# All short matmuls of a step behind its four projections, in a gated recurrent block with a feed-forward gate

## The chip, the cores and the metric

The kernel runs on one core of a Trainium2 chip. Its time is the device time of one execution in microseconds. The time before is the median of three executions. A separate execution was profiled, and every start time and duration below comes from that one.

## The reference

One sequence of 2048 tokens with 512 features goes through a layer norm. An attention-like branch `s` and a feed-forward gate `g` are computed from the normed input, and the output is `x + s * g`. Cut to what matters:

```python
q, k, v = (_causal_dwconv(_silu(x @ W), conv_w) for W, conv_w in ...)  # 4 taps; 16 heads x 128
z, a, b = x @ Wz, x @ Wa, x @ Wb
q, k = rope(q), rope(k)
q = q / max(norm(q), 1e-12);  k = k / max(norm(k), 1e-12)
for s in range(4):                           # each token and the three before it
    attn = einsum('bshd,bshd->bsh', q, lag(k, s)) * scale
    out += (attn * sigmoid(lag(a, s) * b))[..., None] * lag(v, s)
s = (out * rsqrt(mean(out * out) + eps) * norm_w * silu(z)) @ Wout
g = silu(relu(x @ sign(up).T * up_scale) @ sign(down).T * down_scale * output_scale)
```

## The kernel before

**Three stages.** A setup normalizes and transposes x and splits it into a coarse part `x_hi` and a remainder `x_lo`. The attention stage then goes over 16 heads of 128 features. In each head it goes over 4 chunks of 512 tokens. The feed-forward and the output projection follow. Each engine has its own program, written out by hand, and semaphores order them; no scheduler is involved.

**Steps.** The attention stage has one *step* for each head and chunk, counted by `c = h * 4 + g` from 0 to 63, and three more steps that empty the pipeline. A step works on four chunks at once: the newest one, and those one, two and three steps back (`back(h, g, k)`). `front` says that there is a newest chunk, so it is true up to c = 63.

**TensorE in a step**, in the order before:

1. transposes of q and of k of the chunk one step back, 4 of 128x128 each (L829), q into `bank_tqv` and k into `bank_tk`;
2. projections of q and k of the newest chunk. Each projection is a *series* of 12 matmuls of 512 columns on split weights (L771);
3. `turn_v`: 4 transposes of v of the chunk one step back into `bank_tqv` (L798);
4. the projection of v;
5. `sum_values`: the sum of values of the chunk three steps back, 4 or 5 plain fp32 matmuls of up to 132 columns (L808, L813). The trace records each of these as two instructions;
6. the projection of z for the chunk two steps back;
7. two *picks* of 32 columns (L889, L890) and the *scores*, 4 fp32 matmuls of 132 columns (L897, again two records each), for the chunk two steps back.

**The bank that is used twice.** `bank_tqv` holds the transposed q at the start of a step and the transposed v later. ScalarE takes the squares of q out of it for the norms (L556), then `turn_v` may write (`norms_done`), then ScalarE copies the transposed v to `v_tok` (L566). The next step's transposes of q wait for that copy (`v_tok_done`, L824).

**ScalarE in a step**, in the order before: the norms (L556), silu and first convolution tap of q and of k (L521 to L536), the copy to `v_tok` (L566), silu and tap of v, the squares of the summed values (L579), silu of z (L590). In the last chunk of a head it also splits the next head's weights of q, k and v (L516), and in chunk 1 those of z. In step 1 alone it computes a tanh of the gates (L584) ahead of what follows.

**The other engines.** VectorE does the convolutions (L638), the rotation (L648 to L655), the coefficients (L711 to L737) and the gated output (L732). GpSimd computes the inverse norms and `rq_parts`, for which the picks wait (L431 to L445), splits weights (L406), and issues the transfer that adds up the squares (L458).

Of the kernel before, what the change touches and what calls it, by code (L numbers as in the profile page):

```python
# [150 lines left out]
def attention(nc, env):  # L151
# [18 lines left out]
    with ExitStack() as ctx:  # L170
# [4 lines left out]
        v_tok = sb("v_tok", [P, NB, D], at=ctx)  # L175
# [12 lines left out]
        out_sq = sb("out_sq", [P, CH], at=ctx)  # L188
        o_buf = sb("o_buf", [P, 2, CH], at=ctx)
        bank_qv, bank_kz = banks[0], banks[1]  # L190
        bank_tqv, bank_tk = banks[2], banks[3]
        bank_out, bank_rq = banks2
# [66 lines left out]
        turned_v = sem("turned_v", ctx)  # L259
        norms_done = sem("norms_done", ctx)  # L260
        v_tok_done = sem("v_tok_done", ctx)
# [12 lines left out]
        out_done = sem("out_done", ctx)  # L274
        out_sq_done = sem("out_sq_done", ctx)
# [3 lines left out]
        sq_added = sem("sq_added", ctx)  # L279
        block = ctx.enter_context(nc.Block())  # L280

        def back(h, g, k):

            h2, g2 = (h, g - k) if g >= k else (h - 1, g - k + G)
            if isinstance(h2, int) and not 0 <= h2 < H:
                return None
            return h2, g2
# [16 lines left out]
        def is_tail(h, g, step):  # L304

            return isinstance(h, int) and h == H and g == step
# [157 lines left out]
        def _(act):  # L464
# [78 lines left out]
            act.wait_ge(raw_in["z"], 16)  # L543
            nc.scalar.activation(w_hi["z"][:, :, :], raw["z"][:, :, :], ACT.Copy).then_inc(whi_done["z"], 1)

            def step(h, g):
                c = h * G + g
                front = back(h, g, 0)
                if at := back(h, g, 1):
                    g1 = at[1]  # L550
                    wait(act, turned_qk, c)
                    wait(act, rnorm_done, c - 2)
                    for i, bank in enumerate((bank_tqv, bank_tk)):
                        for b in range(BC):
                            block_of = bank[:, b * P:(b + 1) * P]
                            last = nc.scalar.activation(block_of, block_of, ACT.Square,  # L556
                                                        accum_out=norms[:, g1 % 2, i * BC + b:i * BC + b + 1])
                    last.then_inc(norms_done, 1)
                if front and not is_start(h, g):
                    silu_and_tap("q", bank_qv, h, g, c)  # L560
                    silu_and_tap("k", bank_kz, h, g, c)
                if at := back(h, g, 1):
                    g1 = at[1]
                    wait(act, turned_v, c)
                    wait(act, out_done, c - 3)
                    nc.scalar.activation(v_tok[:, g1 * BC:(g1 + 1) * BC, :],  # L566
                                         bank_tqv[:, :].rearrange("p (b d) -> p b d", b=BC),
                                         ACT.Copy).then_inc(v_tok_done, 1)
                if g == 3 and not is_last(h):
                    split_hi("q", h + 1, c)  # L570
                if front:
                    silu_and_tap("v", bank_qv, h, g, c)
                if g == 3 and not is_last(h):
                    split_hi("k", h + 1, c)
                    split_hi("v", h + 1, c)
                if back(h, g, 3):
                    wait(act, out_done, c - 2)
                    wait(act, sq_added, 16 * (c - 3))
                    nc.scalar.activation(out_sq[:, :], bank_out[:, :], ACT.Square).then_inc(out_sq_done, 1)  # L579
                if is_start(h, g - 1):  # L580
                    for i in range(2):
                        part = gate0[:, i * HALF_NB:(i + 1) * HALF_NB, :]
                        act.wait_ge(prod_done, i + 1)
                        nc.scalar.activation(part, part, ACT.Tanh, scale=0.5).then_inc(tanh_done, 1)  # L584
                if at := back(h, g, 2):
                    g2 = at[1]
                    wait(act, proj_done["z"], c - 1)
                    wait(act, o_done, c - 3)
                    bank = bank_qv if is_tail(h, g, 1) else bank_kz
                    nc.scalar.activation(z_act[:, g2 % 2, :], bank[:, :], ACT.Silu).then_inc(z_done, 1)  # L590
                if g == 1 and front and not (isinstance(h, int) and h == 0):
                    split_hi("z", h, c - 2)

# [149 lines left out]
        def _(pe):  # L743
# [33 lines left out]
            for b in range(NB):  # L777
                turn_x(b)
                half = range((b + 1) % 2 * TERMS // 2, ((b + 1) % 2 + 1) * TERMS // 2)
                at = (b + 1) // 2  # L780
# [13 lines left out]
            def turn_v(g1, c):  # L794
                wait(pe, norms_done, c)
                wait(pe, conv_done["v"], 3 * c)
                for b in range(BC):
                    last = nc.tensor.transpose(bank_tqv[:, b * P:(b + 1) * P],  # L798
                                               y["v"][:, g1 % 2, b * P:(b + 1) * P], ident)
                last.then_inc(turned_v, 1)  # L800

            def sum_values(g3, c):

                wait(pe, coef_done, c - 2)
                wait(pe, v_tok_done, c - 2)
                wait(pe, o_done, c - 3)
                if g3 > 0:
                    nc.tensor.matmul(bank_out[:, 0:LAGS], v_tok[:, g3 * BC - 1, :],  # L808
                                     coef[:, (g3 - 1) % 2, BC - 1, P:BW], start=True, stop=False,
                                     skip_group_check=True)  # L810
                for b in range(BC):
                    width = BW if b < BC - 1 else P
                    last = nc.tensor.matmul(bank_out[:, b * P:b * P + width], v_tok[:, g3 * BC + b, :],  # L813
                                            coef[:, g3 % 2, b, 0:width], start=(b == 0 and g3 == 0),
                                            stop=(b == BC - 1), skip_group_check=True)
                last.then_inc(out_done, 1)

            def step(h, g):
                c = h * G + g
                front = back(h, g, 0)  # L820
                at1, at2, at3 = (back(h, g, k) for k in (1, 2, 3))
                if at1:
                    g1 = at1[1]
# [20 lines left out]
                if front and not is_start(h, g):  # L844
                    wait(pe, z_done, c - 2)
                    project("k", bank_kz, h, g, c)
                if at1 and front:
                    turn_v(at1[1], c)
                if front:
                    wait(pe, silu_done["q"], 2 * c + 2)  # L850
                    project("v", bank_qv, h, g, c)
                if is_start(h, g):
# [2 lines left out]
                        last = nc.tensor.transpose(bank_ab[:, b * AB:(b + 1) * AB], ab_t[:, b * P:(b + 1) * P],  # L855
                                                   ident[0:AB, 0:AB])
                    last.then_inc(ab_turned, 1)
                if at3 and front:
                    sum_values(at3[1], c)
                if at2 and not is_tail(h, g, 1):  # L860
                    if front:
                        wait(pe, silu_done["k"], 2 * c + 2)
                    else:
                        wait(pe, z_done, c - 2)
                    project("z", bank_kz, at2[0], at2[1], c - 2)
                if at1 and not front:
                    turn_v(at1[1], c)
                if is_tail(h, g, 0):
                    wait(pe, silu_done["v"], 2 * c)
                    project("z", bank_qv, h - 1, G - 1, c - 1)  # L870
                    sum_values(at3[1], c)
# [8 lines left out]
                if at2:  # L880
# [14 lines left out]
                    for b in range(BC):  # L895
                        at = (g2 * BC + b) * P
# [452 lines left out]
```

## Time and profile before

| | us |
|---|---|
| median of three executions | 1412.47 (1412.08 to 1413.2) |
| the profiled execution, its own time | 1413.44 |
| its span, first to last instruction | 1411.6 |
| TensorE busy in the span | 1377.4 (98%) |
| VectorE / ScalarE / GpSimd busy | 1025.6 / 733.3 / 417.2 |

The attention stage fills the span from about 40 us to 982 us. In the timelines a line merges neighbouring instructions of one kind: its first start, the time from that start to the last one's end, and their count. Matmuls overlap in their records, since each passes through a pipeline. What a piece of work takes of TensorE's time is therefore read from its start to the start of the next piece, not from the duration.

### The profile page before, as it was taken

Reading aid. Unit: us, or ns where it says so; the run is one execution under the profiler, and the core shown is the slowest. Engines: PE = TensorE matmul, PEld = TensorE weight load, DVE = VectorE, ACT = ScalarE, POOL = GpSimd, SP = SyncE. Lnnn points to the kernel's source line nnn. Section 1 sums busy time; section 2 is a strip of 40 time slices with the busy share of each in tenths; the row PEclk is TensorE's granted clock in tenths of the full one; section 3 lists DMA queues with packets and bytes.
Section 4 is the critical chain, followed back from the end, with each engine's and each line's share of the span. In section 5 each row is a group of like instructions: output and inputs, shape, how many; then the busy total and the mean of one; then the engine's idle time right before and its main releaser. Section 6 shows DMA issues by size and latency. Waiting matters only on the chain. (4 is left out here: it accounts for less than half of the span.)

```text
span 1411.6 us, 23209 instructions
## 1 busy us (share of the span) xinstructions
PE 1377.4 (98%) x7048; PEld 1164.4 (82%) x7048; DVE 1025.6 (73%) x1597; ACT 733.3 (52%) x2146; POOL 417.2 (30%) x504
## 2 busy tenths in 40 slices
PE   6999999999999999999999999998899999999998
PEld 4778888888888888888888888886788888888886
DVE  7889999999999999999999999995113322234442
ACT  5655655556655556555565655553554444332221
POOL 6142443434434344444444444432000000000001
PEclk9999999999999999999999999999899999999999
DMA  9123333433344333443334333332431101065454
GB/s 303 38 70 88 90 83 97 99 87 89 79 100 102 75 97 74 104 97 78 93 74 111 89 82 89 82 83 72 137 120 53 45 22 45 25 185 171 142 170 157
DMA packets 103962, 137.60 MB, mean 97 GB/s; under 512 B 11248, under 2 KB 48112, under 8 KB 103664
## 3 DMA queue, kind: packets, MB, share of 16 engines
q1 hardware_dynamic: 94704, 120.28, 29.6%
q0 software_dynamic: 9216, 16.78, 7.0%
q8 instruction: 24, 0.39, 0.1%
q14 instruction: 18, 0.15, 0.0%
HBM read 61.53 MB, written 25.17 MB: 61 GB/s over the span
## 5 line engine op out<-in xcount | busy, mean ns | idle before, releaser
L431 POOL TENSOR_TENSOR rnorm<-norms,neg_half 128x8 f32<-128x8 f32 x64 | 126.2, 1971 | 366.4 <-DVE norms L663 366.4
L556 ACT ACTIVATE bank<-bank 128x128 f32<-128x128 f32 x512 | 133.7, 261 | 86.3 <-PE bank L829 86.3
L638 DVE SCALAR_TENSOR_TENSOR y_v<-u_v,cw_v,y_v 128x512 f32<-128x512 f32 x192 | 172.7, 899 | 6.8
L638 DVE SCALAR_TENSOR_TENSOR y_k<-u_k,cw_k,y_k 128x512 f32<-128x512 f32 x192 | 159.7, 832 | 16.5 <-ACT y_k L536 9.5
L1141 DVE TENSOR_TENSOR hid_lo<-relu,hid_hi 128x512 fp32r<-128x512 f32 x64 | 44.3, 693 | 172.3 <-ACT hid_hi L1087 172.3
L638 DVE SCALAR_TENSOR_TENSOR y_q<-u_q,cw_q,y_q 128x512 f32<-128x512 f32 x192 | 144.2, 751 | 30.0 <-ACT y_q L536 22.3
L1059 POOL TENSOR_TENSOR g_buf<-g_buf,up_raw 128x512 f32<-128x512 f32 x3 | 3.8, 1278 | 402.7 <-DVE g_buf L1162 402.7
L1182 DVE TENSOR_TENSOR hid_lo<-o_raw,hid_hi 128x512 fp32r<-128x512 f32 x64 | 44.3, 692 | 101.4 <-ACT hid_hi L1107 101.4
L1083 ACT ACTIVATE relu<-bank,us_sb 128x512 f32<-128x512 f32 x64 | 44.1, 689 | 121.7 <-PE bank L1222 121.7
L1107 ACT ACTIVATE hid_hi<-o_raw 128x512 fp32r<-128x512 f32 x64 | 40.5, 633 | 121.8 <-PE bank L1252 116.8
L1237 PE MATMUL bank<-down_sign,hid_hi 128*128 128x512 f32 x256 | 99.8, 390 | 0.9 <-DVE hid_lo L1141 0.9
L1252 PE MATMUL bank<-x_hi,hid_hi 128*128 128x512 f32 x256 | 99.7, 390 | 0.2 <-DVE hid_lo L1182 0.2
L1237 PE MATMUL bank<-down_sign,hid_lo 128*128 128x512 f32 x256 | 99.6, 389 | 0.0
L1252 PE MATMUL bank<-x_hi,hid_lo 128*128 128x512 f32 x256 | 99.6, 389 | 0.0
L1252 PE MATMUL bank<-x_lo,hid_hi 128*128 128x512 f32 x256 | 99.6, 389 | 0.0
L556 ACT ACTIVATION_READ_ACCUMULATOR bank<-bank 128x1 f32 x512 | 95.0, 186 | 0.0
L590 ACT ACTIVATE z_act<-bank 128x512 f32<-128x512 f32 x64 | 38.2, 597 | 99.2 <-PE bank L771 99.2
L521 ACT ACTIVATE u_k<-bank 128x512 f32<-128x512 f32 x64 | 38.3, 599 | 82.6 <-PE bank L771 82.6
L458 POOL DMA_DIRECT2D sq_sum<-out_sq x64 | 59.0, 921 | 70.8 <-ACT out_sq L579 64.8
L771 PE MATMUL bank<-x_hi,whi_q 128*128 128x512 f32 x256 | 76.9, 423 | 0.0
L521 ACT ACTIVATE u_v<-bank 128x512 f32<-128x512 f32 x64 | 38.2, 597 | 72.0 <-PE bank L771 72.0
L771 PE MATMUL bank<-x_hi,whi_v 128*128 128x512 f32 x256 | 75.4, 416 | 0.0
(173 smaller groups left out, 3560.9 us busy)
## 6 DMA issues: line engine op xcount, KB each, us to landing
swapped_q<-y_q SPq DMA_DIRECT2D x128, 128.0 KB, 2.3
swapped_k<-y_k SPq DMA_DIRECT2D x128, 128.0 KB, 2.3
sq_sum<-out_sq POOLq DMA_DIRECT2D x64, 256.0 KB, 3.4
o_scratch<-o_buf SPq DMA_DIRECT2D x64, 256.0 KB, 2.5
o_raw<-o_scratch SPq DMA_DIRECT2D x64, 256.0 KB, 3.2
raw_q<-in_wq SPq DMA_DIRECT2D x16, 256.0 KB, 3.1
raw_k<-in_wk SPq DMA_DIRECT2D x16, 256.0 KB, 3.6
raw_v<-in_wv SPq DMA_DIRECT2D x16, 256.0 KB, 4.5
```

Source lines behind the costliest of these rows:

```text
L431: nc.gpsimd.tensor_tensor(rnorm[:, g1 % 2, :], norms[:, g1 % 2, :], neg_half[:, 0:2 * BC], ALU.pow).then_inc(root_done, 1)
L458: nc.gpsimd.dma_start(sq_sum[:, cols(g3)], out_sq[:, :], accum_op=ALU.add).then_inc(sq_added, 16)
L521: nc.scalar.activation(u[n][:, g % 2, HALO:], bank[:, :], ACT.Silu).then_inc(silu_done[n], 1)
L556: last = nc.scalar.activation(block_of, block_of, ACT.Square, accum_out=norms[:, g1 % 2, i * BC + b:i * BC + b + 1])
L638: nc.vector.scalar_tensor_tensor(y[n][:, g % 2, :], u[n][:, g % 2, i:i + CH], cw[n][:, bass.ds(h * TAPS + i, 1)], y[n][:, g % 2, :], ALU.m ...
L771: last = nc.tensor.matmul(bank[:, :], w[n][:, i % KT, :], part[:, i % KT, cols(g)], start=(i == 0), stop=(i == TERMS - 1))
L1083: nc.scalar.activation(relu[:, j % 2, :], up_banks[j % 2][:, :], ACT.Relu, scale=us_sb[:, j:j + 1]).then_inc(relu_done, 1)
L1107: nc.scalar.activation(o_hi[:, h % 2, :], o_raw[:, h % WR, :], ACT.Copy).then_inc(o_hi_done, 1)
L1141: nc.vector.tensor_tensor(hid_lo[:, j % 2, :], relu[:, j % 2, :], hid_hi[:, j % 2, :].bitcast(fp32), ALU.subtract).then_inc(hid_lo_done, 1)
L1182: nc.vector.tensor_tensor(o_lo[:, h % 2, :], o_raw[:, h % WR, :], o_hi[:, h % 2, :].bitcast(fp32), ALU.subtract).then_inc(o_lo_done, 1)
L1237: last = nc.tensor.matmul(acc[b], part[:, j % 2, b * P:(b + 1) * P], down_sign[:, j, :], start=(j == 0 and part is hid_hi), stop=(j == FT ...
L1252: last = nc.tensor.matmul(sums[b], part[:, h % 2, b * P:(b + 1) * P], wo_tile(w, h // KT, h % KT), start=(h == 0 and k == 0), stop=(h == H ...
```

## The change

Only TensorE's and ScalarE's programs change. No operation is added or removed.

On TensorE, `turn_v` and `sum_values` move behind the projection of z in every step with a newest chunk. The four projections q, k, v, z then stand in a row, and behind them `turn_v`, `sum_values`, picks and scores. On ScalarE, the copy to `v_tok` and the squares move behind silu of z in those steps. The steps that empty the pipeline keep their order.

```diff
+            def copy_v(g1, c):
+                wait(act, turned_v, c)
+                wait(act, out_done, c - 3)
+                nc.scalar.activation(v_tok[:, g1 * BC:(g1 + 1) * BC, :],
+                                     bank_tqv[:, :].rearrange("p (b d) -> p b d", b=BC),
+                                     ACT.Copy).then_inc(v_tok_done, 1)
+
+            def square_out(c):
+                wait(act, out_done, c - 2)
+                wait(act, sq_added, 16 * (c - 3))
+                nc.scalar.activation(out_sq[:, :], bank_out[:, :], ACT.Square).then_inc(out_sq_done, 1)
...
                     silu_and_tap("k", bank_kz, h, g, c)
-                if at := back(h, g, 1):
-                    g1 = at[1]
-                    wait(act, turned_v, c)
-                    wait(act, out_done, c - 3)
...
+                if back(h, g, 1) and not front:
+                    copy_v(back(h, g, 1)[1], c)
...
-                if back(h, g, 3):
-                    wait(act, out_done, c - 2)
-                    wait(act, sq_added, 16 * (c - 3))
-                    nc.scalar.activation(out_sq[:, :], bank_out[:, :], ACT.Square).then_inc(out_sq_done, 1)
+                if back(h, g, 3) and not front:
+                    square_out(c)
...
                     nc.scalar.activation(z_act[:, g2 % 2, :], bank[:, :], ACT.Silu).then_inc(z_done, 1)
+                if back(h, g, 1) and front:
+                    copy_v(back(h, g, 1)[1], c)
+                if back(h, g, 3) and front:
+                    square_out(c)
...
                     project("k", bank_kz, h, g, c)
-                if at1 and front:
-                    turn_v(at1[1], c)
                 if front:
                     wait(pe, silu_done["q"], 2 * c + 2)
                     project("v", bank_qv, h, g, c)
...
-                if at3 and front:
-                    sum_values(at3[1], c)
...
                     project("z", bank_kz, at2[0], at2[1], c - 2)
-                if at1 and not front:
+                if at1:
                     turn_v(at1[1], c)
+                if at3 and front:
+                    sum_values(at3[1], c)
```

On TensorE in a full step, from the end of the projection of k to the first pick, before:

```order
L771 MATMUL bank<-x_lo,whi_k 128x512 x4
L798 MATMUL bank<-const,y_v 128x128 x4
L771 MATMUL bank<-x_hi,whi_v 128x512 x4
L771 MATMUL bank<-x_hi,wlo_v 128x512 x4
L771 MATMUL bank<-x_lo,whi_v 128x512 x4
L808 MATMUL bank<-coef,v_tok 128x4
L813 MATMUL bank<-coef,v_tok 128x132 x3
L813 MATMUL bank<-coef,v_tok 128x128
L771 MATMUL bank<-x_hi,whi_z 128x512 x4
L771 MATMUL bank<-x_hi,wlo_z 128x512 x4
L771 MATMUL bank<-x_lo,whi_z 128x512 x4
L889 MATMUL bank<-rq_parts,sel_r 128x32
```

The same stretch now (`y_v` is v after its convolution, `coef` the coefficients, `whi` and `wlo` the parts of the weights; the change shifts line numbers, L771 is now L780, L798 L807, L813 L822, L889 L896):

```order
L780 MATMUL bank<-x_lo,whi_k 128x512 x4
L780 MATMUL bank<-x_hi,whi_v 128x512 x4
L780 MATMUL bank<-x_hi,wlo_v 128x512 x4
L780 MATMUL bank<-x_lo,whi_v 128x512 x4
L780 MATMUL bank<-x_hi,whi_z 128x512 x4
L780 MATMUL bank<-x_hi,wlo_z 128x512 x4
L780 MATMUL bank<-x_lo,whi_z 128x512 x4
L807 MATMUL bank<-const,y_v 128x128 x4
L817 MATMUL bank<-coef,v_tok 128x4
L822 MATMUL bank<-coef,v_tok 128x132 x3
L822 MATMUL bank<-coef,v_tok 128x128
L896 MATMUL bank<-rq_parts,sel_r 128x32
```

The transposes of v and the sum of values have left the places ahead of and behind the projection of v and stand together ahead of the picks.

On ScalarE in the same step, from the tap of k to the next step's norms, before:

```order
L536 ACTIVATE y_k<-u_k,cw_k 128x512
L566 ACTIVATE v_tok<-bank 128x512
L521 ACTIVATE u_v<-bank 128x512
L531 ACTIVATE u_v<-bank 128x3
L536 ACTIVATE y_v<-u_v,cw_v 128x512
L579 ACTIVATE out_sq<-bank 128x512
L590 ACTIVATE z_act<-bank 128x512
L556 ACTIVATE bank,norms<-bank 128x128 x8
```

The same stretch now (here L556 is the squares, and the norms are L568):

```order
L536 ACTIVATE y_k<-u_k,cw_k 128x512
L521 ACTIVATE u_v<-bank 128x512
L531 ACTIVATE u_v<-bank 128x3
L536 ACTIVATE y_v<-u_v,cw_v 128x512
L595 ACTIVATE z_act<-bank 128x512
L549 ACTIVATE v_tok<-bank 128x512
L556 ACTIVATE out_sq<-bank 128x512
L568 ACTIVATE bank,norms<-bank 128x128 x8
```

The copy to `v_tok` and the squares now come behind silu of z, directly ahead of the next step's norms.

## Rows read from the trace of the kernel before

**Rows 1.** The profile's page: the span, and each engine's busy time and share

```profile
span 1411.6 us, 23209 instructions
...
PE 1377.4 (98%) x7048; PEld 1164.4 (82%) x7048; DVE 1025.6 (73%) x1597; ACT 733.3 (52%) x2146; POOL 417.2 (30%) x504
```

**Rows 2.** Groups of TensorE instructions, 100 to 950 us: busy time, mean ns, idle

```profile
L771 PE MATMUL bank<-x_hi,whi_v 128*128 128x512 f32 x236 | 69.6, 416 | 0.0
...
L771 PE MATMUL bank<-x_hi,whi_k 128*128 128x512 f32 x232 | 62.0, 389 | 0.0
```

**Rows 3.** Timeline of TensorE in one full step: start, duration, instructions merged

```profile
504.75 1.07 PE L771 MATMUL bank<-x_hi,whi_k 128*128 128x512 f32 x4
...
507.48 0.60 PE L798 MATMUL bank<-const,y_v 128*128 128x128 f32 x4
507.83 1.18 PE L771 MATMUL bank<-x_hi,whi_v 128*128 128x512 f32 x4
...
510.69 0.28 PE L808 MATMUL bank<-coef,v_tok 128*128 128x4 f32 x2
...
511.72 1.18 PE L771 MATMUL bank<-x_hi,whi_z 128*128 128x512 f32 x4
...
514.59 0.18 PE L889 MATMUL bank<-rq_parts,sel_r 128*128 128x32 f32 x1
...
514.73 1.15 PE L897 MATMUL bank<-rot_q,rot_k 128*128 128x132 f32 x8
515.72 0.60 PE L829 MATMUL bank<-const,y_q 128*128 128x128 f32 x4
516.15 0.60 PE L829 MATMUL bank<-const,y_k 128*128 128x128 f32 x4
...
519.35 1.07 PE L771 MATMUL bank<-x_hi,whi_k 128*128 128x512 f32 x4
```

**Rows 4.** Timeline of TensorE in the pipeline's last steps

```profile
972.85 0.28 PE L808 MATMUL bank<-coef,v_tok 128*128 128x4 f32 x2
...
973.88 0.26 PE L889 MATMUL bank<-rq_parts,sel_r 128*128 128x32 f32 x1
...
974.11 1.15 PE L897 MATMUL bank<-rot_q,rot_k 128*128 128x132 f32 x8
975.10 0.95 PE L115 MATMUL bank<-ones,sq_sum 128*128 128x2 f32 x8
```

**Rows 5.** Timeline of ScalarE in the step of rows 3

```profile
509.10 0.58 ACT L566 ACTIVATE v_tok<-bank 128x512 f32<-128x512 f32 x1
...
514.79 0.60 ACT L590 ACTIVATE z_act<-bank 128x512 f32<-128x512 f32 x1 [1.91 <-PE bank L771]
```

**Rows 6.** Timeline of VectorE in the step of rows 3

```profile
510.74 2.54 DVE L638 SCALAR_TENSOR_TENSOR y_k<-u_k,cw_k,y_k 128x512 f32<-128x512 f32 x3
```

**Rows 7.** Waits between 100 and 950 us: total us, times, longest

```profile
DVE y_q L638 <- ACT y_q L536: 15.9, 14, 1.2
```

**Rows 8.** Timeline of TensorE in steps 1 to 3

```profile
59.89 0.60 PE L829 MATMUL bank<-const,y_q 128*128 128x128 f32 x4
...
75.78 0.40 PE L889 MATMUL bank<-rq_parts,sel_r 128*128 128x32 f32 x1 [2.96 <-POOL rq_parts L441]
...
83.61 0.62 PE L771 MATMUL bank<-x_hi,whi_k 128*128 128x512 f32 x2
```

**Rows 9.** Timeline of ScalarE at the end of step 1

```profile
61.46 1.14 ACT L584 ACTIVATE gate<-gate 128x512 f32<-128x512 f32 x2
```

**Rows 10.** Timeline of GpSimd in step 2

```profile
75.18 0.55 POOL L441 TENSOR_TENSOR rq_parts<-rq_x,rq_parts 128x16 fp32r<-128x16 f32 x1
```

**Rows 11.** Busy time by stretch: length, PE, PEld, DVE, ACT, POOL, granted clock, DMA share, GB/s

```profile
76.00:82.00 6.00, 6.00 (x24) 5.52 (x25) 4.55 (x9) 1.92 (x14) 0.00 (x0) 0.50 0.00 0
...
972.90:979.60 6.70, 6.60 (x57) 6.21 (x55) 3.41 (x9) 1.86 (x4) 1.18 (x3) 1.00 0.33 78
```

More of the change, by code:

```diff
@@ L561, in step @@
                     silu_and_tap("k", bank_kz, h, g, c)
-                if at := back(h, g, 1):
-                    g1 = at[1]
-                    wait(act, turned_v, c)
-                    wait(act, out_done, c - 3)
-                    nc.scalar.activation(v_tok[:, g1 * BC:(g1 + 1) * BC, :],
-                                         bank_tqv[:, :].rearrange("p (b d) -> p b d", b=BC),
-                                         ACT.Copy).then_inc(v_tok_done, 1)
+                if back(h, g, 1) and not front:
+                    copy_v(back(h, g, 1)[1], c)
                 if g == 3 and not is_last(h):
```

## The prediction

> **What bounds the kernel now.** I read the page first: TensorE is busy for 98% of the span [rows 1], so only its own time and its few stalls count. Then its groups of instructions [rows 2]. The first four matmuls of v's projection take 416 ns each in the mean, those of k's 389 ns, though both do the same work, and neither group has idle time ahead of it. What differs is what stands before them: transposes before v, a projection before k. Last the timeline of a full step [rows 3], where I take start-to-start times. Step 3 and all up to step 63 have this form. That makes 61 full steps.
>
> **The price of a switch, from rows.** In the step of [rows 3] the projection of k, which follows another projection, lasts from 504.75 to 507.48, or 2.73 us. The transposes of v and the projection of v together last from 507.48 to 510.69, or 3.21 us. Four transposes among other short matmuls take 516.15 - 515.72 = 0.43 us. If v's projection ran as k's does, the pair would take 0.43 + 2.73 = 3.16 us. Entering the projection from the transposes thus costs 0.05 us more than the two pieces alone.
>
> The sum of values, the projection of z and the two picks last from 510.69 to 514.73, or 4.04 us. In the new order z follows a projection, 2.73 us. For a sum that is followed directly by the picks there is a place in the trace, the pipeline's last steps [rows 4]: the sum lasts from 972.85 to 973.88, or 1.03 us, and the picks behind it from 973.88 to 974.11, or 0.23 us, not the 0.14 us (514.59 to 514.73) that they take behind a projection. Together 2.73 + 1.03 + 0.23 = 3.99 us, so this switch is worth 0.05 us too.
>
> **The change part by part.**
>
> *Projections in a row, TensorE.* Two entries into a projection go, 0.05 + 0.05 = 0.10 us in each full step. 61 steps give 6.1 us. Steps 1 and 2 lose the entry into v alone, 0.1 us in sum. The starts are read to 0.01 us, so a step's gain is uncertain by some 0.02 us, or 1.2 us in all. Together -6.2 us.
>
> *The sum behind the transposes of v.* The trace has no fp32 sum directly behind transposes. The nearest rows are the sum behind a projection [rows 3] and the picks and scores behind a sum [rows 4]. At best it costs nothing more. At worst it pays what the picks pay behind a sum, 0.23 - 0.14 = 0.09 us, or 5.5 us over 61 steps, with no later gain to set against it. Less than nothing I exclude, since the sum was counted as it runs behind a projection, its shortest place. I take zero, because in [rows 4] each of three pieces of short matmuls follows the last with no more than that 0.09 us, which is already in the sum. The other end stays for the range.
>
> *The copy to `v_tok`, ScalarE.* It leaves the middle of the step, where the next user of the bank was half a step away, and now the next step's transposes of q follow soon. Let T be the end of z's projection, where `turn_v` now starts. Silu of z starts 514.79 - 514.59 = 0.20 us behind T and takes 0.60 us [rows 3, 5], so ScalarE is free at T + 0.8. The four transposes of v end at T + 0.6 (their 0.60 us in [rows 3]). The copy takes 0.58 us [rows 5] and ends at about T + 1.4. The next transposes of q come at T + 0.43 + 1.03 + 0.23 + 0.99 = T + 2.68, the last term being the scores, 515.72 - 514.73. So 1.3 us are left, and the copy costs nothing while ScalarE comes to it in time. In chunk 3 of a head two weight splits of about 0.6 us each stand ahead of silu of z. They fall into z's projection, 2.73 us, beside the 1.3 us of v's silu and tap, and still fit.
>
> *The squares, ScalarE.* They follow the copy, when the sum is there: T + 0.43 + 1.03 and about 0.2 us of pipeline, so they run from T + 1.7 to T + 2.3. The norms, queued behind them, can start only at T + 2.68 + 0.79, when all eight transposes are done. GpSimd waits for the squares to issue its transfer, and behind that wait stand only the inverse norms, whose input comes after the norms. In chunk 1 the split of z's weights is queued behind the squares; it moves to about T + 2.9, half a step or more ahead of its use. All at nothing.
>
> *VectorE.* It is behind TensorE by several us in [rows 6]: the convolution of k ends at 513.28. Its user, the transposes at 515.72 and 516.15, keeps 2.4 us of slack. In 850 us VectorE waits for ScalarE's tap of q 14 times [rows 7], about once a head, so it catches up each head and doesn't become the bound when a head gets 0.4 us shorter. `turn_v` and the sum ask for its results later than before.
>
> *Step 1, the one place where the copy is late.* Step 1 has no projection of z. `turn_v` stands behind v's projection there and ends near 59.8 us. On ScalarE the copy is now queued behind silu and tap of v and behind the tanh of the gates, which ends at 62.60 [rows 9]. With 0.58 us for the copy, `v_tok_done` comes at 63.15 instead of well ahead, and the transposes of q, at 59.89 before [rows 8], start 3.3 us later. But step 2 has had a stall of its own, 2.96 us ahead of the picks, until GpSimd's `rq_parts` at 75.73 [rows 8, 10]. GpSimd's chain doesn't move: it was started by the gates. From 63.15, step 2 needs 0.79 + 2.84 for transposes and q and 3 x 2.73 for the rest, so z ends at 74.97, `turn_v` at 75.40, and the picks still go at 75.78. The new stall replaces the old one.
>
> *The clock around the stall.* After the old stall the granted clock is 0.50, the 1.2 GHz level, for 76 to 82 us, and 1.00 again later [rows 11]. From the picks at 75.78 to k's projection at 83.61 [rows 8] TensorE takes 7.83 us. The same stretch of a normal step, 514.59 to 519.35, takes 4.76 us [rows 3]. A fall costs 3.07 us. The new stall of 3.3 us is as long as the old one, so I expect the fall to move with it: z then ends at 74.97 + 3.07 = 78.04, the picks go at 78.5 at full clock, and the old stall is gone. Before, their equivalent was 75.78 + 3.07 = 78.85. The start gains 0.4 us.
>
> **Sum.** -6.2 - 0.4 = -6.6 us. Against the profiled execution that is 1413.44 - 6.6 = 1406.8. The median of the runs lies 0.97 us lower, so the forecast is 1412.47 - 6.6 = **1405.9 us**.
>
> **A rule that speaks against it.** In the last steps TensorE ran short fp32 matmuls alone, some of 2 columns, between 972.9 and 979.6 us, and the granted clock stayed at 1.00, the 2.4 GHz level [rows 11]. So the longer run of short matmuls per step, now 2.68 + 0.79 = 3.5 us, should not lower it. The Trainium skill ("TensorE: Matmul & The Clock Gate", Part 4, PE-mode transpose) says that transposes don't count as TensorE being busy in the way matmuls do. Twelve of the 32 short instructions are transposes here, and none of those in the rows of the last steps are, so the trace doesn't quite settle it. It enters as rival E.
>
> **The rivals.**
>
> B, the clock holds. If the stall in step 1 doesn't bring the clock down, the picks go at 75.78 at full clock and the whole 3.07 us are gained: -6.2 - 3.1 = -9.3, 1403.2 us. For it: the stall lies between two stretches of work in another phase than the old one. Against: it is longer than the one that brought the clock down.
>
> C, the switch moves instead of going. If the sum behind transposes pays its 0.09 us, 0.10 - 0.09 = 0.01 us a step is left: -0.6 - 0.4 = -1.0, 1411.4 us, no change that can be seen. This is also the case that the change doesn't do what it says. A part of it, half the payment, gives about 1408.7 us.
>
> D, the bank's round trip, slower. The transposes of q at each step's start wait for the copy. It decides once ScalarE is over 1.3 us late with it, and above 1.4 us it costs more than the 0.10 us gained. If ScalarE came 2 us late in each step, 61 x (0.7 - 0.1) = +37, 1449 us. For it: the slack is the smallest in the step, where half a step was to spare. Against: ScalarE is idle for 1.91 us just ahead of silu of z [rows 5].
>
> E, the clock falls in the long run of short matmuls, slower. Once a step at 3.07 us it would be 61 x 3.07 - 6 = +181, 1594 us. Against it stands [rows 11].
>
> **How the numbers follow.** A, the forecast, 0.55. B 0.22. C in full 0.12, a part of it 0.04. D 0.04. E 0.03. About 0.2% or 2.8 us is what a measurement can tell from no change. Faster by more than that are A, B and the part of C: 0.81. Within it is C: 0.12. Slower are D and E: 0.07. A range from 1402.7 to 1408.9 holds A, B and the part of C, 0.81, with the 1.2 us of reading error in it.
>
> **What would show it right or wrong.** The profile after should have v's and z's projections at 2.73 us each and their first four matmuls at about 389 ns, as k's; a full step from one q transpose to the next shorter by 0.10 us; no idle TensorE ahead of the q transposes from step 3 on; a stall of about 3.3 us at 60 us, none ahead of the picks at 75 us, and half the clock around 62 to 69 us. The sum behind the transposes of v should last 1.03 us up to the picks; at 1.12 us it is C. A wait of the q transposes for the copy to `v_tok` in every step is D. The prediction is wrong if a step isn't shorter by 0.08 to 0.12 us.

## The result and the profile after

| | us |
|---|---|
| median before, beside it | 1412.47 |
| median after, five executions | 1404.7 (1404.29 to 1406.68) |
| ratio, with its 95% interval | 0.9945 (0.9932 to 0.9958) |
| profiled execution, its own time: before, after | 1413.44, 1404.7 |

The change gains 7.8 us, where 6.6 us were forecast. The time lies within the range, between case A (1405.9) and case B (1403.2). The profile after is read beside the rows of before. First the groups of TensorE instructions between 100 and 950 us (busy time, mean ns of one, idle ahead):

```profile
L780 PE MATMUL bank<-x_hi,whi_q 128*128 128x512 f32 x236 | 69.0, 414 | 0.0
...
L780 PE MATMUL bank<-x_hi,whi_z 128*128 128x512 f32 x236 | 63.1, 389 | 0.0
...
L780 PE MATMUL bank<-x_hi,whi_v 128*128 128x512 f32 x236 | 63.1, 389 | 0.0
L780 PE MATMUL bank<-x_hi,whi_k 128*128 128x512 f32 x236 | 63.1, 389 | 0.0
```

The first four matmuls of v's projection took 416 ns each and k's 389 [rows 2]. Now v, z and k all stand at 389, and only q, which still follows short matmuls, is at 414. The difference of two such means is a sign of the fee and not its size: four times 27 ns are 0.11 us, while the starts give about 0.05, because the first matmul of the series also starts sooner behind the last transpose, as is shown below. A full step on TensorE's timeline answers to [rows 3]:

```profile
513.85 1.07 PE L780 MATMUL bank<-x_hi,whi_k 128*128 128x512 f32 x4
...
516.57 1.07 PE L780 MATMUL bank<-x_hi,whi_v 128*128 128x512 f32 x4
...
519.29 1.07 PE L780 MATMUL bank<-x_hi,whi_z 128*128 128x512 f32 x4
...
522.02 0.60 PE L807 MATMUL bank<-const,y_v 128*128 128x128 f32 x4
522.45 0.28 PE L817 MATMUL bank<-coef,v_tok 128*128 128x4 f32 x2
...
523.49 0.26 PE L896 MATMUL bank<-rq_parts,sel_r 128*128 128x32 f32 x1
...
523.72 1.15 PE L904 MATMUL bank<-rot_q,rot_k 128*128 128x132 f32 x8
524.71 0.60 PE L838 MATMUL bank<-const,y_q 128*128 128x128 f32 x4
```

The projections take 2.72, 2.72 and 2.73 us, the transposes of v 0.43, the sum 1.04, the picks 0.23 and the scores 0.99. For the length of a step, here are the q transposes that open step 4 and those that close step 63, in the profile before and then after:

```profile
94.32 0.60 PE L829 MATMUL bank<-const,y_q 128*128 128x128 f32 x4
...
966.02 0.60 PE L829 MATMUL bank<-const,y_q 128*128 128x128 f32 x4
```

```profile
92.03 0.60 PE L838 MATMUL bank<-const,y_q 128*128 128x128 f32 x4
...
957.13 0.60 PE L838 MATMUL bank<-const,y_q 128*128 128x128 f32 x4
```

That is 871.70 / 60 = 14.528 us a step before and 865.10 / 60 = 14.418 after, 0.110 us less. At the first of these starts the kernel was 2.3 us ahead already. ScalarE behind the end of z's projection at 522.02:

```profile
522.22 0.60 ACT L595 ACTIVATE z_act<-bank 128x512 f32<-128x512 f32 x1 [1.26 <-PE bank L780]
522.71 0.59 ACT L549 ACTIVATE v_tok<-bank 128x512 f32<-128x512 f32 x1
523.85 0.60 ACT L556 ACTIVATE out_sq<-bank 128x512 f32<-128x512 f32 x1 [0.55 <-PE bank L822]
```

The copy ends at 523.30, 1.4 us ahead of the q transposes at 524.71. All of TensorE's waits between 60 and 950 us are two, and both stand at the start:

```profile
PE bank L838 <- ACT v_tok L549: 3.1, 1, 3.1
PE bank L896 <- POOL rq_parts L441: 0.8, 1, 0.8
```

```profile
63.34 0.66 PE L838 MATMUL bank<-const,y_q 128*128 128x128 f32 x4 [3.11 <-ACT v_tok L549]
...
76.55 0.28 PE L896 MATMUL bank<-rq_parts,sel_r 128*128 128x32 f32 x1 [0.77 <-POOL rq_parts L441]
```

The stall of 2.96 us ahead of the picks [rows 8] is down to 0.77, and a stall of 3.11 us stands at the start of step 2. At the start the clock does not fall in this execution. The stretch that had 0.50 before [rows 11] now has 1.00:

```profile
76.00:82.00 6.00, 5.45 (x33) 4.89 (x34) 5.37 (x11) 3.22 (x18) 1.02 (x3) 1.00 0.02 5
```

Both profiles also have a fall at the end of the attention stage, from 983 us before and from 973 us after, and TensorE idles there for some 11 us ahead of the feed-forward. From the q transposes that close step 63 to the end of the span both take the same time, 445.6 and 445.7 us.

### The profile page after: what moved, and what is told of

Same layout as the page of the kernel before. It is cut to its first block and busy times, and to the rows that moved or that the text cites. A ratio compares the mean times of both kernels' runs of the same rounds, so it can differ in the third digit from the quotient of the medians.

```text
span 1402.9 us, 23209 instructions
## 1 busy us (share of the span) xinstructions
PE 1368.7 (98%) x7048; PEld 1162.9 (83%) x7048; DVE 1026.8 (73%) x1597; ACT 741.3 (53%) x2146; POOL 409.2 (29%) x504
## 5 line engine op out<-in xcount | busy, mean ns | idle before, releaser
L568 ACT ACTIVATE bank<-bank 128x128 f32<-128x128 f32 x512 | 134.0, 262 | 79.2 <-PE bank L838 79.2
L647 DVE SCALAR_TENSOR_TENSOR y_v<-u_v,cw_v,y_v 128x512 f32<-128x512 f32 x192 | 158.9, 828 | 6.9
L568 ACT ACTIVATION_READ_ACCUMULATOR bank<-bank 128x1 f32 x512 | 95.7, 187 | 0.0
L780 PE MATMUL bank<-x_hi,whi_q 128*128 128x512 f32 x256 | 75.8, 418 | 0.0
L904 PE MATMUL bank<-rot_q,rot_k 128*128 128x132 f32 x512 | 73.7, 285 | 0.0
L822 PE MATMUL bank<-coef,v_tok 128*128 128x132 f32 (+1 forms) x512 | 71.9, 283 | 0.0
```

What stands on the lines that cost most here:

```text
L647: nc.vector.scalar_tensor_tensor(y[n][:, g % 2, :], u[n][:, g % 2, i:i + CH], cw[n][:, bass.ds(h * TAPS + i, 1)], y[n][:, g % 2, :], ALU.m ...
L780: last = nc.tensor.matmul(bank[:, :], w[n][:, i % KT, :], part[:, i % KT, cols(g)], start=(i == 0), stop=(i == TERMS - 1))
L904: last = nc.tensor.matmul(scores[:, b, :], rot["k"][:, at:at + P], rot["q"][:, at:at + BW], start=True, stop=True)
```

## The experiments

Two theories stood against each other on the full steps. **Theory 1**: each entry from short matmuls into a projection costs a fee, and the change takes away two of three per step. **Theory 2**: the gain comes from joining the short matmuls, or the fee grows with the short work ahead of it. For the start, the question was whether the stall was moved or added, and what the clock makes of it. The diffs are against the changed kernel unless the text says otherwise. "Full step" is the mean of steps 4 to 63, from the starts of the q transposes as above.

| run | median us | ratio to before (95%) | full step us | entries a step |
|---|---|---|---|---|
| before | 1412.5 to 1413.2 | | 14.528 | 3 |
| changed kernel | 1404.7 | 0.9945 (0.9932 to 0.9958) | 14.418 | 1 |
| e0_after_again | 1405.34 | 0.9945 (0.9931 to 0.9958) | 14.418 | 1 |
| e1_turn_only | 1408.09 | 0.9969 (0.9957 to 0.9981) | 14.468 | 2 |
| e2_sum_only | 1410.13 | 0.9981 (0.9972 to 0.999) | 14.477 | 2 |
| e5_turn_halves | 1407.44 | 0.9954 (0.9938 to 0.9971) | 14.473 | 2 |
| e8_turn_twice | 1411.07 | 0.9983 (0.9973 to 0.9993) | 14.498 | 3 |
| e3_step1_kept | 1406.66 | 0.9955 (0.9941 to 0.9968) | 14.418 | 1 |
| e4_step1_only | 1411.94 | 0.9995 (0.9986 to 1.0004) | 14.528 | 3 |
| e6_copy_first | 1403.76 | 0.9932 (0.9915 to 0.9948) | 14.418 | 1 |
| e7_copy_last | 1431.32 | 1.0123 (1.0106 to 1.014) | 14.826 | 1 |
| e10_gate_wait | 1407.45 | 0.9961 (0.9947 to 0.9975) | 14.528 | 3 |
| e9_best | 1401.44 | 0.9917 (0.9903 to 0.9931) | 14.419 | 1 |

**Each move alone.** Of the changed kernel, the first run takes the sum and the squares back:

```diff
-                if back(h, g, 3) and not front:
+                if back(h, g, 3):
                     square_out(c)
...
-                if back(h, g, 3) and front:
-                    square_out(c)
...
+                if at3 and front:
+                    sum_values(at3[1], c)
                 if at2 and not is_tail(h, g, 1):
...
                     turn_v(at1[1], c)
-                if at3 and front:
-                    sum_values(at3[1], c)
```

> Only the transposes of v (and on ScalarE their copy) move behind the projection of z; the sum of values and the squares stay where they were. Theory 1, entries into a projection: the pair of transposes and projection of v took 3.209 us a step before and should take 0.437 + 2.720 = 3.157, so 0.05 us a step or 3.2 us over 62 steps go, and the start gains some 2.5 us as in the changed kernel, since step 1 now stalls at 60 us instead of step 2 at 73 us: about 1406.8 us. Theory 2, the gain comes with the joined run of all short matmuls only: 1412.5 - 2.5 = 1410.0 us. v's series at 2.72 us and z's still near 2.85 us under theory 1.

The second takes the transposes of v and their copy back, in the same manner.

> Only the sum of values (and on ScalarE the squares) moves behind the projection of z; the transposes of v stay ahead of v's projection. Theory 1: sum, z and picks took 4.025 us before and should take 2.726 + 1.036 + 0.223 = 3.985, 0.04 us a step or 2.4 us over 61 steps, no gain at the start: about 1410.0 us. Theory 2, the gain needs the joined run: 1412.5 us. The projection of q got 0.02 us shorter in the changed kernel without any change ahead of it; where that shows again (here or in the kernel with the transposes alone) tells which move it comes from, and would add 1.3 us.

The two leave the fee where theory 1 says. The transposes' move frees v, the sum's move frees z, and each leaves the other's first matmuls as they were. Groups of e1_turn_only, 100 to 950 us:

```profile
L778 PE MATMUL bank<-x_hi,whi_z 128*128 128x512 f32 x236 | 69.3, 415 | 0.0
...
L778 PE MATMUL bank<-x_hi,whi_v 128*128 128x512 f32 x232 | 62.0, 389 | 0.0
```

and of e2_sum_only:

```profile
L778 PE MATMUL bank<-x_hi,whi_v 128*128 128x512 f32 x236 | 69.5, 416 | 0.0
...
L778 PE MATMUL bank<-x_hi,whi_z 128*128 128x512 f32 x236 | 63.1, 389 | 0.0
```

Their full steps are 0.060 and 0.052 us shorter than before, together 0.112, and both moves at once give 0.110. So the moves add up, and joining all short matmuls brings nothing more in sum. The median of e2_sum_only was forecast at 1410.0 and came at 1410.13. That of e1_turn_only was forecast at 1406.8 and came at 1408.09: its steps gain 0.060 us, where 0.05 were forecast, so the miss is not there. Its profiled execution took 1406.2 us, with a stall of 3.1 us in step 1 and no fall of the clock. What the other five lost has no profile.

**More entries, no more work.** The transposes of v in two halves (`turn_v` gets the blocks that it turns, and signals behind the last one):

```diff
                     project("k", bank_kz, h, g, c)
+                if at1 and front:
+                    turn_v(at1[1], c, range(2))
...
-                    turn_v(at1[1], c)
+                    turn_v(at1[1], c, range(2, BC) if front else range(BC))
```

> The changed kernel, with the four transposes of v split: two stand ahead of v's projection, two behind z's. No instruction is added; each step enters a projection from short matmuls twice instead of once. Theory 1, a fixed fee for each entry: the full step goes from 14.418 back up by 0.055 to about 14.47 us, the same as with all four transposes there; 1404.7 + 3.4 = 1408.1 us. Theory 2, the fee grows with the short work that stands ahead of the projection: half of it, 14.445 us a step, 1406.3 us.

Measured 14.473, the number of theory 1, though half as much short work stands there. Part of this match is chance. Taken from the starts of single instructions, as means over steps 4 to 63, only 0.032 of the 0.055 us lie in the transposes and the projection of v. The projection of q takes 0.017 more (2.844 instead of 2.827), and that of k, which short matmuls follow again, 0.006.

In e8_turn_twice the second half stands ahead of z's projection instead of behind it.

> The changed kernel, with two transposes of v ahead of v's projection and two ahead of z's, none behind it. Three entries into a projection in a step, as before the change, with the sum of values still behind z. Theory 1: two fees of 0.055 more, 14.418 + 0.11 = 14.53 us a step, as in the kernel before, though the sum is moved and each run of transposes is short; about 1404.7 + 6.7 = 1411.4 us. Theory 2, the fee grows with the short work: 14.418 + 0.055 = 14.47 us, 1408 us.

Measured 14.498, 0.080 above the changed kernel, between the 0.11 of theory 1 and the 0.055 of theory 2. The fee is no single number, then. To compare entries I take the short piece and its projection together, less 0.109 us for each transpose and 2.720 us for a projection in a row, and less another 0.006 us where short matmuls follow the projection, since its last matmul then takes that much longer. The fee is 0.047 us for v behind four transposes (before), 0.034 behind two (e5_turn_halves) and 0.033 (e8_turn_twice), and 0.025 for z behind two there. For v, two transposes cost some 70% of what four cost, which speaks against a fee in proportion to the short work; for z they cost about half of v's four, which does not. So the entries count, and the short work ahead changes the fee of each. Neither theory holds in its pure form.

The starts also show where the fee is paid. In the profile before, the first matmul of v starts 28 ns behind the last transpose and the second 314 ns behind the first. That is 342 ns, where 109 + 227 = 336 would pass without a switch. The switch itself is nearly free. The rest lies in the matmuls from the second to about the tenth, which start 224 to 236 ns apart and not 227. What slows them is not shown. That they meet the work of another engine at that time is a rival that no run here varies.

**The start.** First the changed kernel with step 1 alone in its old place:

```diff
                     project("k", bank_kz, h, g, c)
+                if is_start(h, g - 1):
+                    turn_v(at1[1], c)
...
-                if at1:
+                if at1 and not is_start(h, g - 1):
                     turn_v(at1[1], c)
```

> The changed kernel, but step 1 alone keeps the old place of the transposes of v and of their copy. Theory 1, the start gains only because the stall moved to step 1 and the clock held there: the stall is back ahead of the picks of step 2 at about 3.2 us, the clock falls to 0.50 behind it, and the time is 1404.7 + 2.5 = 1407.2 us. Rival, the start's gain comes from the shorter steps or by chance of the run: 1404.7 us, no fall of the clock.

The stall is back at 2.99 us ahead of the picks, and the clock falls behind it:

```profile
76.59 0.28 PE L898 MATMUL bank<-rq_parts,sel_r 128*128 128x32 f32 x1 [2.99 <-POOL rq_parts L441]
```

```profile
77.30:80.70 3.40, 3.40 (x17) 3.31 (x16) 3.26 (x7) 0.50 (x4) 0.00 (x0) 0.51 0.00 0
```

The fall lasts half as long as in the profile before, where it filled 76 to 82 us [rows 11]. The median is 1406.66, where 1407.2 were forecast. The kernel before with the new step 1 is the counterpart. It stalled for 3.12 us in step 1 and for 0.73 us ahead of the picks, its clock held in the profiled execution, and the median came out 0.7 us lower, within the interval:

> The kernel before, but step 1 alone has the new order (transposes of v behind v's projection, their copy behind the tanh). Theory 1: the stall of 3.1 us moves from step 2 to step 1, the clock holds, and the time is 1412.5 - 2.5 = 1410.0 us with the full steps as before (14.58 us in the mean). Rival, the stall in step 1 adds to the old one: 1412.5 + 3.1 = 1415.6 us; or the clock falls here too: 1412.1 us.

So the stall is moved and not added. (Its expectation gives the full step before as 14.58 us; it is 14.528.) The gain in the median is smaller than the 2.5 us that the two profiles suggested. One reason is that the fall behind a stall differs between executions, in whether it comes and in how long it lasts. The changed kernel run again showed the first:

> The changed kernel again, beside the next two on the same chip, so that these can be compared with it: 1404.7 us within some 1 us, a full step of 14.418 us.

Its profile has the same 3.11 us stall, now with a fall behind it (the stretches during and behind the stall; the granted clock is the third number from the end):

```profile
60.00:63.80 3.80, 0.99 (x7) 0.62 (x5) 3.73 (x7) 2.84 (x6) 0.00 (x0) 1.00 0.31 72
63.80:67.20 3.40, 3.10 (x12) 2.81 (x13) 3.33 (x6) 1.34 (x9) 0.00 (x0) 0.51 0.35 96
```

What this fall cost can be read from the starts of the q transposes of step 2 and of `turn_v`, here and then in the profile after:

```profile
64.10 1.12 PE L838 MATMUL bank<-const,y_q 128*128 128x128 f32 x4 [3.11 <-ACT v_tok L549]
...
77.46 0.60 PE L807 MATMUL bank<-const,y_v 128*128 128x128 f32 x4
```

```profile
63.34 0.66 PE L838 MATMUL bank<-const,y_q 128*128 128x128 f32 x4 [3.11 <-ACT v_tok L549]
...
75.18 0.60 PE L807 MATMUL bank<-const,y_v 128*128 128x128 f32 x4
```

Work that took 11.84 us takes 13.36, so this fall costs 1.5 us, half of the 3.07 that was read from the longer one before. Some of it is hidden: the wait for `rq_parts` that follows is gone. The table adds up steps 1 to 3, from their first q transposes to those of step 4, in single profiled executions:

| run | first q transposes at us | steps 1 to 3, us | stalls of TensorE, us | fall behind a stall |
|---|---|---|---|---|
| before | 46.83 | 47.50 | 0.3, 2.96 | 6.8 us long |
| changed kernel | 47.05 | 44.98 | 3.11, 0.77 | none |
| e0_after_again | 47.82 | 45.48 | 3.11 | 3.4 us long |
| e4_step1_only | 46.17 | 45.09 | 3.12, 0.73 | none |
| e10_gate_wait | 46.79 | 41.32 | 0.3 | none |
| e9_best | 46.98 | 41.17 | 0.3 | none |

The same kernel with and without the fall differs by 0.5 us here. Of the 1.1 us between its two profiles, 0.8 lie ahead of step 1, in the setup. In the profiled executions of all runs step 1's transposes start between 46.2 and 48.3 us, so one profile is a poor measure of anything under 2 us at the start.

Next the stall split in two, with the copy ahead of the tanh in step 1:

```diff
                 if is_start(h, g - 1):
+                    copy_v(back(h, g, 1)[1], c)
                     for i in range(2):
...
-                if back(h, g, 1) and front:
+                if back(h, g, 1) and front and not is_start(h, g - 1):
```

> The changed kernel, but in step 1 ScalarE copies the transposed v ahead of the tanh instead of behind it. Theory 1: the stall at 60 us shrinks from 3.1 to about 1.8 us, since the copy then follows the tap of v at 61.3 us; the tanh's user on VectorE comes only at 67.7 us, so nothing is late; the stall ahead of the picks of step 2 grows from 0.8 to about 1.8 us, because GpSimd's chain is bound by the gates and not by TensorE. Total idle time stays near 3.7 us less the 0.5 us by which VectorE came late: 1404.2 to 1404.7 us, clock held at 1.00. Rival, if the stall of step 1 is the bound: 1403.4 us.

The stalls became 1.61 and 1.71 us, 3.3 in sum instead of 3.9, about as forecast. The median is 1403.76, between the 1404.2 of the expectation and the 1403.4 of its rival. One of its four executions, the profiled one, had a fall all the same, behind the stall of 1.71 us, and took 1407.66. So half the length does not make a stall safe, and whether falls are rarer so stays open.

Last the stall itself. GpSimd waits for the gates ahead of all its steps, but only one operation of step 1 uses them:

```diff
-            pool.wait_ge(gate_done, 2)
             pool.wait_ge(cleared, 6)
...
                     wait(pool, gates_done, c - 3)
+                    if is_start(h, g - 1):
+                        pool.wait_ge(gate_done, 2)
```

In the kernel before, this alone:

> The kernel before; only GpSimd's wait for the gates stands later, ahead of the one operation of step 1 that uses them, instead of ahead of all its steps. Theory: the 2.96 us stall ahead of the picks of step 2 is the whole cause of the clock's fall at 75 us. GpSimd then has the inverse norms of step 2 at about 73 us instead of 75.7, the stall goes or is under 0.5 us, the clock holds at 1.00, full steps stay at 14.528 us: 1412.6 - 2.8 - 1.4 to 3.1 = 1406.7 to 1408.4 us. Rival, the clock falls there for another reason (the fp32 scores and transposes): 1409.8 us.

Measured 1407.45, in the range of the forecast. GpSimd's `rq_parts` is there at 72.25, and the picks follow z's projection without a wait at 72.64:

```profile
71.70 0.55 POOL L440 TENSOR_TENSOR rq_parts<-rq_x,rq_parts 128x16 fp32r<-128x16 f32 x1
```

```profile
72.64 0.18 PE L890 MATMUL bank<-rq_parts,sel_r 128*128 128x32 f32 x1
```

```profile
76.00:82.00 6.00, 6.00 (x30) 4.94 (x29) 5.79 (x12) 4.20 (x16) 1.16 (x1) 1.00 0.01 3
```

No wait is left ahead of the picks and the clock is 1.00 where it was 0.50, with the same scores and transposes in the same place. The profiles of the other runs say the same. With a stall of 1.7 to 3.0 us ahead of these picks the clock fell behind them (before, e2_sum_only, e3_step1_kept, e6_copy_first). With none or under 0.8 us it did not (changed kernel, e1_turn_only, e4_step1_only, e5_turn_halves, e9_best, e10_gate_wait). The other three had their fall in step 2 and none here. So the stall brings the fall, and not the scores and transposes. With its 5.5 us this one wait is worth some 70% of the whole change.

**The bank's round trip**, overdrawn by putting the copy behind the squares:

```diff
-                if back(h, g, 1) and front:
-                    copy_v(back(h, g, 1)[1], c)
                 if back(h, g, 3) and front:
                     square_out(c)
+                if back(h, g, 1) and front:
+                    copy_v(back(h, g, 1)[1], c)
```

> The changed kernel, but on ScalarE the copy of the transposed v stands behind the squares instead of ahead of them. This makes the bank's round trip the bound: with T the end of z's projection, the squares run to T + 2.3 and the copy to T + 2.9 us, while TensorE wants the bank at T + 2.69. Theory 1, the slack of about 1.2 us in the changed kernel is real and is now overdrawn by 0.2 us: the full step is 14.418 + 0.2 = 14.6 us, a wait of that size ahead of the q transposes for the copy in every step, 1404.7 + 13 = 1418 us, slower than before. Rival, the slack is larger than read: no wait, 1404.7 us.

The step is 0.41 us longer, not 0.2, and the median is 1431.32 us, not 1418. The kernel is slower than before. One step of it, TensorE and then ScalarE:

```profile
521.72 0.60 PE L807 MATMUL bank<-const,y_v 128*128 128x128 f32 x4
...
523.42 1.15 PE L904 MATMUL bank<-rot_q,rot_k 128*128 128x132 f32 x8
524.77 0.43 PE L838 MATMUL bank<-const,y_q 128*128 128x128 f32 x2 [0.20 <-ACT v_tok L549]
```

```profile
523.56 0.60 ACT L556 ACTIVATE out_sq<-bank 128x512 f32<-128x512 f32 x1 [0.96 <-PE bank L822]
524.05 0.59 ACT L549 ACTIVATE v_tok<-bank 128x512 f32<-128x512 f32 x1
```

The copy ends at 524.64 and the transposes start at 524.77, where without a wait they would start 0.99 us behind the scores, at 524.41. The profile calls 0.20 us of that idle. The rest, up to 0.36, is the record of the last score, which nothing overlaps now. From the copy's end to the transposes' start 0.13 us pass. The four transposes then take 0.49 us instead of 0.43 in the mean.

**Both together.** The changed kernel with step 1 in its old place and GpSimd's wait later:

> The changed kernel with step 1 in its old place and with GpSimd's wait for the gates later, so that neither the stall of step 1 nor that of step 2 is left. Full steps 14.418 us as in the changed kernel; of its 3.1 and 0.8 us of stalls at the start nothing is left, the clock holds: 1404.7 - 3.9 = 1400.8 us. Rival, the start is bound by another chain (VectorE's convolutions run without a break from 58 to 78 us): a stall reappears ahead of the transposes of step 3, 1403 us.

Measured 1401.44 us, 0.9917 of before, where 1400.8 were forecast. It beats both kernels. The full steps are those of the changed kernel, TensorE's only wait at the start is 0.28 us for k's convolution, and the clock holds.

## Why the prediction was right, and where it was off

**The two entries: right, and the number is closer than its parts.** Forecast 0.10 us a step, measured 0.110. v's and z's projections run at k's pace, as the text asked. The reading error of 0.02 us a step covers the difference. Over 61 steps it makes 6.7 us and not 6.1. The parts of the 0.110, as means over steps 4 to 63, are 0.052 for the transposes and v, as read, and 0.036 for the sum, z and the picks, where 0.05 was read. For these the step of [rows 3] has 4.04 us; the mean of the steps with five matmuls in the sum is 4.03, and where the sum has four the switch was cheaper still. The other 0.022 come from two projections ahead of which nothing changed, and which the sum had at nothing.

**Terms that were missing: the projections of q and k.** k's takes 2.720 us instead of 2.726, because no short matmuls follow it now. q's takes 2.827 instead of 2.843. With the transposes moved alone it is 2.838 and with the sum alone 2.842, so most of this gain comes only when both moves are made. Ahead of it stand the same transposes as before, and its matmuls from the second to the tenth are the ones that start closer together. Why wasn't found. That the total came within 0.01 us of the forecast is thus in part luck: z's term was too large by 0.014 and these two made up for it. Against that, the sum costs 0.005 us more than read.

**The sum behind the transposes, rival C: refuted.** It lasts 1.04 us (522.45 to 523.49), not 1.12.

**The copy and the squares: right.** The copy was forecast to end 1.4 us and ended 1.28 us behind z's end, with 1.41 us to spare. The squares end 2.4 us behind it. Rival D was a real danger and not the case here. Its turning point was read well: with 1.41 us to spare, less the 0.13 us from the copy's end to the next transpose in e7_copy_last, the copy could come 1.28 us later, and the text says 1.3. There the copy's end comes 0.23 us behind the time at which TensorE would have gone on, and the step pays 0.41 us: 0.13 more for the release, 0.05 for slower transposes, and little else. Here the expectation of 0.2 us failed, since it counted only what was late.

**The clock in the long run of short matmuls, rival E: not the case.** From 522.0 to 525.5 us TensorE ran all 32 short instructions of a step, twelve of them transposes, and the clock there is 1.00, as it is over the whole stretch:

```profile
100.00:950.00 850.00, 850.00 (x4690) 735.37 (x4689) 797.90 (x1242) 515.05 (x1708) 353.95 (x415) 1.00 0.38 91
522.00:525.50 3.50, 3.50 (x34) 3.48 (x32) 3.43 (x6) 2.20 (x4) 0.46 (x1) 1.00 0.33 75
```

The Trainium skill ("TensorE: Matmul & The Clock Gate", Part 4, PE-mode transpose) holds that transposes don't count as TensorE being busy in the way matmuls do. This trace doesn't contradict that, but in a run that mixes them with fp32 matmuls it made no difference.

One place speaks for more care with short matmuls. Behind the last full step TensorE has nothing else to run, and waits in between. There the clock of the profile after falls at 973.2 us, with two instructions of the last sum still to come:

```profile
972.00:973.10 1.10, 1.09 (x9) 1.10 (x10) 0.00 (x0) 0.00 (x0) 0.00 (x0) 1.00 0.85 268
973.20:984.00 10.80, 0.27 (x2) 0.00 (x0) 0.75 (x1) 0.60 (x1) 0.85 (x1) 0.50 0.33 70
```

Before, it fell only when TensorE was idle, and the prediction's row of 972.9 to 979.6 us at 1.00 [rows 11] is right for that execution.

**The start: the stall right, the clock a mixture.** The stall of step 1 was forecast at 3.3 us and is 3.11. The statement "GpSimd's chain doesn't move" was off: `rq_parts` is ready at 76.49 instead of 75.73, so 0.77 us of the old stall remain. Of these 0.76 us, 0.2 were there before step 1 began, since the setup ended later. The rest is in GpSimd's own operations: from the first inverse norm to `rq_parts` of step 2 they take 7.70 us (68.79 to 76.49) instead of 7.17 (68.56 to 75.73). Why is not shown. Case A (the fall moves along) against case B (the clock holds) was put as either the one or the other. The two profiles of the changed kernel show one of each, with 1404.7 and 1405.82 us, and the fall makes only 0.5 us of that difference. The price of a fall, 3.07 us, came from the one profile of before, where it lasted 6.8 us. In e3_step1_kept and in e0_after_again it lasted half as long. The gain at the start was therefore mis-sized in both cases: with 6.7 us for the steps, the other 1.1 us of the median's 7.8 go to the start and to what differs between executions, between A's 0.4 and B's 3.1.

## What to carry to other kernels

Where an engine is busy for 98% of the span, look for groups that do the same work at different mean durations: 416 against 389 ns with no idle time ahead was the whole case. Take the size from starts, not from these durations. Put matmuls of one kind in a row, and count the entries first; the short work ahead changes the fee of each, but not in proportion throughout. Before work is moved to the end of a step, count the round trip through each buffer that the next step's first instruction needs, and expect a wait to cost more than what is late: 0.41 us for 0.23 here. A single early stall can cost nearly as much as a fee in every step (5.5 against 6.7 us), once for its length and once for the clock behind it.

## What the runs showed of the hardware

- A matmul series of 512 columns in split fp32 runs at 0.2267 us each (2.720 / 12) when it follows another such series. Behind two or four fp32 transposes it pays 0.025 to 0.047 us once, nearly all of it in its matmuls from the second to the tenth (e8_turn_twice, before).
- A wait that is released 0.23 us late cost 0.41 us of TensorE's time (e7_copy_last).
- A stall of about 3 us at the 2.4 GHz level was followed by a fall to the 1.2 GHz level in some executions and in others not, with the same kernel and the same stall (3.11 us in both profiles of the changed kernel). Falls lasted 3.4 us (e0_after_again, e3_step1_kept) or 6.8 us (before, e7_copy_last), and one came behind a stall of 1.71 us (e6_copy_first).
- In the full steps, runs of 3.5 us with short fp32 matmuls and transposes alone did not lower the clock: it is 1.00 from 100 to 950 us.
